# A spline stage on one core: the third power on GpSimd, three quarters of the near part on TensorE, and a new order of the steps

## The chip, the core and the metric

One NeuronCore of a Trainium2 chip runs the whole program. TensorE multiplies matrices, VectorE, ScalarE and GpSimd work elementwise, SyncE (SP) issues most DMAs; each engine runs its own queue in order, and semaphores tie the queues together. The metric is the device time of one launch in microseconds (us), the median of several runs.

## What is computed

`x` is 32 x 64 x 56 x 56, float32. Two 3x3 convolutions with the signs of the weights, each followed by a batch norm, then the residual sum; on its result a cubic spline with 32 knots, whose control values differ by channel (a rank-8 mix). Cut to what matters:

```python
out = relu(batchnorm(conv3x3(x, sign(w1))))
out = relu(batchnorm(conv3x3(out, sign(w2))) + x)          # input v of the spline
u = (clip(v * a + b, -1.5, 1.5) + 1) * 0.5 * 31
i = floor(u); t = clip(u - i, 0, 1)
spline = table[i-1] * b0(t) + table[i] * b1(t) + table[i+1] * b2(t) + table[i+2] * b3(t)
y = id_gain * v + einsum("bchwr,cr->bchw", spline, mix) + bias
```

## The kernel before

A stage of convolutions (to about 408 us of the span) writes its output to scratch memory in HBM. The change lies, but for a few constants, in the second stage, the function `spline`. It handles 32 chunks, each of 128 partitions (two images of 64 channels) by 1568 pixels, half an image pair. Of each pixel, the position on the knots in fixed point (`place`, then `offset`, the signed offset from the next even knot times 2^25, and `cell`, the number of the cell in bfloat16) is formed, and five tables give the coefficients of a polynomial in the offset: T_NEAR, T_FAR, T_SQ, T_LIN, T_VAL. A coefficient is read from its table without a gather: TensorE multiplies 0/1 or sign masks ("is the cell at or above a threshold") by the steps of the table, and so sums up to the right entry. The far term is in |offset| - 1, clipped at 0.

Chunk c passes through these steps. Names are those of the code, lines those of the profile:

- SP: `load(c)` reads y into `lin` (L959); `spread(c)` (L969) waits for `cell_ready` and issues sixteen SBUF to SBUF copies, which lay the cells of 32 channels at a time over all partitions (`cell4`), 98 KB each; `store(c)` (L975) writes `lin` out after `whole`.
- ScalarE: `scale` (L1016), `position` (L1027), `cells` (L1038), `distance` (|offset|, L1064), `far_distance` (L1070), `far_square` (L1076), `distance_square` (L1083), and `edge(c, q)` (L1089), two sign masks of 4 x 1568 columns. `edge` waits on `copied`, that is for all sixteen copies of its chunk.
- VectorE: `fixed` (L1177), `offsets` (L1185), `linear` (L1171), `middle(c, q)` (L1192), the two other masks, which wait for the same copies; then, each reading a table from PSUM, `near_cube` (L1212), `far_cube` (L1219), `square` (L1233), `slope` (L1241), `value` (L1254), and `far_part` (L1226), `add_slope` (L1247) and `finish` (L1261), which read SBUF alone.
- GpSimd: `add_x` (L999) and `add_far` (L1004) issue DMAs that add x and the far part into `lin`.
- TensorE: `table(c, t)` (`product`, L1334), 128 matmuls of 392 columns for each of T_NEAR and T_FAR, 64 for each of the others, and `add_near_part` (L1344), float32 matmuls with the identity `ident` that add `poly` onto the square table in PSUM, for four quarters (`sub`) of the chunk. Two PSUM buffers `tab` alternate: table t waits until table t-2 has been consumed (`table_used`).

The order on each engine is written out by hand. On ScalarE, for chunk index c of the loop: position(c+2), far_distance(c), scale(c+3), far_square(c), distance_square(c), cells(c+2), both edge masks of c+1, distance(c+1). The waits that tie it to the copies are these:

```python
def edge(c, q):
    act.wait_ge(copied[c % 2], copies(c))
def spread(c):
    sp.wait_ge(cell_ready, c + 1)
```

## Time and profile before

| | us |
|---|---|
| median of 3 runs (lowest to highest) | 1127.5 (1126.77 to 1128.81) |
| the profiled execution: its time | 1126.34 |
| its span in the trace | 1124.5 |
| TensorE busy in the span | 1074.4 |
| VectorE busy | 963.5 |
| ScalarE busy | 899.2 |
| GpSimd busy | 170.2 |

The profile is one execution. Busy time counts the instructions of an engine; a matmul record is one pass (float32 matmuls leave two), and the ends of matmuls are modelled. A timeline row merges neighbouring instructions of one kind (x2, x16) and gives start and duration. The duration of a DMA issue on SP is that of issuing; landing is told apart. On ScalarE and VectorE an instruction may start some 0.1 us before its predecessor's end, so start-to-start times are a little shorter than durations.

### The profile page before, as it was taken

What the parts mean: (1) busy time and instruction counts of PE and PEld (TensorE: products, weight loads), DVE (VectorE), ACT (ScalarE), POOL (GpSimd) and SP (SyncE); (2) the same over time, 40 slices, a digit from 0 to 9 for tenths busy, and PEclk for the clock granted to TensorE, in tenths of its full rate; (3) what the DMA queues carried; (4) which work ended last, traced back from release to release, by engine and by line L of the source; (5) the groups of instructions that cost most, each with busy time, mean ns of one, the idle gap of its engine ahead of it and who ended that gap; (6) DMA issues with size and microseconds to landing.
All of it is one profiled execution on the core that took longest, in us unless ns stands there. A gap on an engine that the chain in (4) does not pass through costs nothing.

```text
span 1124.5 us, 53088 instructions
## 1 busy us (share of the span) xinstructions
PE 1074.4 (96%) x24602; PEld 751.0 (67%) x24602; DVE 963.5 (86%) x931; ACT 899.2 (80%) x410; POOL 170.2 (15%) x236
## 2 busy tenths in 40 slices
PE   6999999799999968899999999999999999999996
PEld 5777777687777745566677666666666666666674
DVE  4865666686767779999999999999999999999986
ACT  4444544686777648999999999999999999999970
POOL 8388200000000000111011011110110111101100
PEclk9999999899999989999999999999999999999999
DMA  8577774777677946788888888889988888888642
GB/s 278 216 286 281 278 261 169 266 279 292 252 286 291 350 169 156 191 212 239 227 223 241 219 220 250 218 213 237 230 227 232 230 225 219 235 221 227 169 125 87
DMA packets 57335, 259.43 MB, mean 231 GB/s; under 512 B 15952, under 2 KB 15952, under 8 KB 49104
## 3 DMA queue, kind: packets, MB, share of 16 engines
q1 hardware_dynamic: 48368, 208.39, 52.1%
q0 software_dynamic: 8640, 48.17, 23.6%
q8 instruction: 147, 2.41, 0.9%
q10 hardware_dynamic: 160, 0.30, 0.1%
q14 instruction: 20, 0.16, 0.0%
HBM read 104.28 MB, written 77.07 MB: 161 GB/s over the span
## 4 chain that ended last, share of the span: by engine, by line
PE 94%; DVE 3%; issue 1%; DMA 1%; ACT 0%; ACTq 0%; DVEq 0%
PE tab L1334 52%; PE acc L771 34%; PE tab L1344 8%; DMA w_raw<-in_w 1%; DVE middle_mask L1192 0%; DVE far_sq L1241 0%; PE tab L1356 0%; DVE poly L1233 0%; DVE lin L1276 0%; DVE poly L1272 0%; DVE middle_mask L1201 0%; DVE stats L581 0%; ACT zbuf L1044 0%; DVE edge_mask L1201 0%; DVE offset L1185 0%
## 5 line engine op out<-in xcount | busy, mean ns | idle before, releaser
L1334 PE MATMUL tab<-edge_mask,diag 128*32 128x392 bf16 x10240 | 453.0, 329 | 9.7 <-issue 4.3
L1334 PEld LDWEIGHTS tab<-edge_mask,diag 128*32 128x32 f16 x10240 | 297.5, 97 | 153.5 <-issue 16.3
L1089 ACT ACTIVATE edge_mask<-cell,thr 128x6272 bf16<-128x6272 bf16 x62 | 338.8, 5513 | 2.1 <-DMA cell<-cell 2.1
L472 ACT ACTIVATE yout<-acc 128x1568 f32<-128x1568 f32 x64 | 94.5, 1477 | 162.9 <-PE acc L771 142.3
L771 PE MATMUL acc<-split,w 64*64 64x385 f16 (+3 forms) x4608 | 192.2, 327 | 11.5 <-DVE w L520 10.3
L771 PE MATMUL acc<-band_split,w 64*64 64x385 f16 (+3 forms) x4608 | 192.7, 327 | 6.5 <-DVE band_split L540 3.6
L599 DVE BATCH_NORM_STATS2 stats<-yout 128x392 f32 (+1 forms) x240 | 118.1, 556 | 93.1 <-ACT yout L472 93.1
L1334 PE MATMUL tab<-middle_mask,diag 128*32 128x392 bf16 x4096 | 187.2, 329 | 1.9 <-DVE middle_mask L1201 1.0
L771 PEld LDWEIGHTS acc<-split,w 64*64 64x64 f16 x4608 | 143.9, 108 | 59.0 <-issue 12.8
L771 PEld LDWEIGHTS acc<-band_split,w 64*64 64x64 f16 x4608 | 149.3, 108 | 49.6 <-issue 4.9
L1334 PEld LDWEIGHTS tab<-middle_mask,diag 128*32 128x32 f16 x4096 | 119.2, 97 | 56.7 <-issue 2.4
L1004 POOL DMA_DIRECT2D lin<-far x32 | 50.1, 1564 | 650.4 <-DVE far L1226 650.4
L1192 DVE TENSOR_SCALAR middle_mask<-cell,thr 128x6272 bf16<-128x6272 bf16 x62 | 114.6, 1848 | 0.0
L1344 PE MATMUL tab<-poly,ident 128*32 128x392 f32 x1024 | 92.7, 492 | 0.0
L999 POOL DMA_DIRECT2D lin<-in_x x28 | 32.3, 1153 | 257.7 <-ACT lin L1016 257.7
L1212 DVE SCALAR_TENSOR_TENSOR poly<-tab,first,poly 128x1568 f32<-128x1568 f32 x31 | 57.4, 1851 | 15.6 <-PE tab L1334 15.6
L1344 PEld LDWEIGHTS tab<-poly,ident 128*32 128x32 f32 x1024 | 46.1, 110 | 29.8 <-issue 16.5
L572 DVE SCALAR_TENSOR_TENSOR split<-split,xin 128x3136 f16<-128x3136 f16 (+4 forms) x19 | 55.0, 2907 | 10.1 <-ACT split L462 10.0
L1233 DVE SCALAR_TENSOR_TENSOR poly<-tab,first,dist_sq 128x1568 f32<-128x1568 f32 x31 | 57.3, 1848 | 3.8 <-PE tab L1344 3.6
L1226 DVE SCALAR_TENSOR_TENSOR far<-far,cst,far_sq 128x1568 f32<-128x1568 f32 x32 | 59.3, 1852 | 1.2
L1219 DVE SCALAR_TENSOR_TENSOR far<-tab,first,far 128x1568 f32<-128x1568 f32 x31 | 57.4, 1851 | 2.1 <-PE tab L1334 1.7
L1064 ACT ACTIVATE poly<-offset 128x1568 f32<-128x1568 int32 x32 | 48.4, 1513 | 12.7 <-DVE offset L1185 12.4
(151 smaller groups left out, 1013.7 us busy)
## 6 DMA issues: line engine op xcount, KB each, us to landing
y_scratch<-yout SPq DMA_DIRECT2D x32, 1568.0 KB, 6.1
cell<-cell SPq DMA_DIRECT2D x496, 98.0 KB, 4.0
xin<-y_scratch SPq DMA_DIRECT2D x16, 1568.0 KB, 6.2
lin<-far POOLq DMA_DIRECT2D x32, 784.0 KB, 8.6
out<-lin SPq DMA_DIRECT2D x31, 784.0 KB, 5.0
xin<-in_x SPq DMA_DIRECT2D x15, 1568.0 KB, 6.7
lin<-y_scratch SPq DMA_DIRECT2D x30, 784.0 KB, 8.4
lin<-in_x POOLq DMA_DIRECT2D x28, 784.0 KB, 8.3
```

The costliest lines, as they stand in the source:

```text
L472: act.activation(yout[b][:, :].rearrange("p (r k x) -> p k r x", r=2, k=TILES)[:, 2 * part:2 * part + 2], acc[:, 4 * part:4 * part + 4, 0: ...
L572: dve.scalar_tensor_tensor(out=inner(split[b][1], first, end), in0=inner(split[b][0], first, end), scalar=-SPLIT, in1=rows(xin[b], first, ...
L599: dve.bn_stats(stats[:, bass.ds(COUNTS * (g - base) + t, 1), :], yout[b][:, own]).then_inc(counted, 1)
L771: mm = pe.matmul(to[:, top:end, cols], weights[part][own, tap * C:(tap + 1) * C], image[own, first + dy + top:first + dy + end, from_cols] ...
L1089: act.activation(mask_of(c, q)[:, :, :], cell4[c % 2][:, :, :], ACT.Sign, bias=thr[:, q:q + 1]).then_inc(sign_mask_ready, 1)
L1192: dve.tensor_scalar(mask_of(c, q)[:, :, :], cell4[c % 2][:, :, :], thr[:, q:q + 1], None, ALU.is_ge).then_inc(mask_ready, 1)
L1212: dve.scalar_tensor_tensor(out=quarters(poly[c % 2]), in0=summed(c, T_NEAR), scalar=base(c, T_NEAR), in1=quarters(poly[c % 2]), op0=ALU.ad ...
L1219: dve.scalar_tensor_tensor(out=quarters(far[c % 2]), in0=summed(c, T_FAR), scalar=base(c, T_FAR), in1=quarters(far[c % 2]), op0=ALU.add, o ...
L1226: dve.scalar_tensor_tensor(out=far[c % 2][:, :], in0=far[c % 2][:, :], scalar=cc(AMP), in1=far_sq[:, :], op0=ALU.mult, op1=ALU.mult).then_ ...
L1233: dve.scalar_tensor_tensor(out=quarters(poly[c % 2]), in0=summed(c, T_SQ), scalar=base(c, T_SQ), in1=quarters(dist_sq), op0=ALU.add, op1=A ...
L1334: mm = pe.matmul(tab[(c + t) % 2][j * GROUP:(j + 1) * GROUP, sub, 0:SUB], keep["diag"][part][:, j % 2, t, q, :], mask_of(c, q)[:, j, sub * ...
L1344: mm = pe.matmul(tab[(c + T_SQ) % 2][j * GROUP:(j + 1) * GROUP, sub, 0:SUB], keep["ident"][:, j * GROUP:(j + 1) * GROUP], poly[c % 2][:, s ...
```

## The change

- GpSimd multiplies the clipped far distance by its square (`far_third(c + 1)`, once the middle masks of that chunk are written), one chunk ahead; for chunk 0 VectorE does it. `far_part` goes. The amplitude, made a power of four, enters by its root as the scale of `far_square`, so `add_far` sends what `far_cube` leaves.
- The near table is signed and is multiplied by `offset` instead of |offset|; `ident` holds 2^-25 instead of 1. `distance` writes into `far`.
- TensorE adds the near part for three quarters of a chunk. For the fourth VectorE adds it in the second instruction of `square`, and `rest_of_square` multiplies by the squared distance.
- `slope` writes over `offset`.
- The order is new. ScalarE: position(c+2), scale(c+3), distance_square(c), first edge mask of c+1, distance, far_distance and far_square of c+1, cells(c+2), second edge mask of c+1. VectorE: rest_of_square, add_slope, value and finish of c-1, near_cube(c), offsets(c+1), fixed and linear of c+2, far_cube(c), both middle masks of c+1, square(c), slope(c). SP issues the store ahead of the spread.

The diff, cut to its core (the declarations of the new semaphores are left out):

```diff
-WIDEN = 256.0
+HALF_EXPONENT = 59.5
+PE_QUARTERS = 3
...
-            link(pool.affine_select(out=keep["ident"][:, :], in_=keep["ident"][:, :], compare_op=ALU.not_equal, fill=1.0,
+            link(pool.affine_select(out=keep["ident"][:, :], in_=keep["ident"][:, :], compare_op=ALU.not_equal, fill=1 / POINT,
...
+                bits = amax[:, :].bitcast(I32)
+                link(dve.tensor_scalar(bits, bits, 23, None, ALU.logical_shift_right), chain)
+                link(dve.tensor_scalar(bits, bits, 0.5, HALF_EXPONENT, ALU.mult, ALU.add), chain)
+                link(dve.tensor_scalar(bits, bits, 23, None, ALU.logical_shift_left), chain)
+                link(dve.tensor_copy(col(ROOT_AMP), amax[:, 0:1]), chain)
+                link(dve.tensor_tensor(amax[:, :], amax[:, :], amax[:, :], ALU.mult), chain)
                 link(dve.reciprocal(inv[:, :], amax[:, :]), chain)
-                link(dve.tensor_scalar(inv[:, :], inv[:, :], WIDEN, None, ALU.mult), chain)
                 link(dve.tensor_copy(col(INV_AMP), inv[:, 0:1]), chain)
-                link(dve.tensor_scalar(col(AMP), amax[:, 0:1], 1 / WIDEN, None, ALU.mult), chain)
+                link(dve.tensor_copy(col(AMP), amax[:, 0:1]), chain)
...
-                    link(dve.tensor_tensor(coef[:, :, T_NEAR, at], knots(bend, 1 + 2 * start, count, 4),
-                                           square, ALU.subtract), chain)
+                    beside = knots(bend, 1 + 2 * start, count, 4)
+                    right, left = (square, beside) if start else (beside, square)
+                    link(dve.tensor_tensor(coef[:, :, T_NEAR, at], right, left, ALU.subtract), chain)
...
+        def sloped(c):
+            return offset[c % 2][:, :].bitcast(F32)
...
                 if c + 4 < CHUNKS:
                     load(c + 4)
+                if c > 0:
+                    store(c - 1)
                 if c + 2 < CHUNKS:
                     spread(c + 2)
-                if c > 0:
-                    store(c - 1)
...
+            def far_third(c):
+                pool.wait_ge(mask_ready, dve_masks(c))
+                pool.wait_ge(far_sq_ready, c + 1)
+                pool.tensor_tensor(far[c % 2][:, :], far[c % 2][:, :], far_sq[:, :],
+                                   ALU.mult).then_inc(far_third_ready, 1)
             def add_far(c):
-                pool.wait_ge(far_part_ready, c + 1)
+                pool.wait_ge(table_used, used(c, T_FAR))
+                pool.wait_ge(lin_ready, c + 1)
                 pool.dma_start(lin_of(c)[:, :], far[c % 2][:, :], accum_op=ALU.add).then_inc(far_added, 16)
             for c in range(CHUNKS):
                 if AHEAD <= c + 3 < CHUNKS:
                     add_x(c + 3)
                 add_far(c)
+                if c + 1 < CHUNKS:
+                    far_third(c + 1)
...
             def distance(c):
                 act.wait_ge(offset_ready, c + 1)
-                wait_past(act, whole, c - 1)
-                act.activation(poly[c % 2][:, :], offset[c % 2][:, :], ACT.Abs, scale=1 / POINT).then_inc(dist_ready, 1)
+                wait_past(act, far_added, 16 * (c - 1))
+                act.activation(far[c % 2][:, :], offset[c % 2][:, :], ACT.Abs, scale=1 / POINT).then_inc(dist_ready, 1)
             def far_distance(c):
                 act.wait_ge(dist_ready, c + 1)
-                wait_past(act, far_added, 16 * (c - 1))
-                act.activation(far[c % 2][:, :], poly[c % 2][:, :], ACT.Relu, bias=cc(MINUS_1)).then_inc(far_ready, 1)
+                act.activation(far[c % 2][:, :], far[c % 2][:, :], ACT.Relu, bias=cc(MINUS_1)).then_inc(far_ready, 1)
             def far_square(c):
                 act.wait_ge(far_ready, c + 1)
-                wait_past(act, slope_ready, c)
-                act.activation(far_sq[:, :], far[c % 2][:, :], ACT.Square).then_inc(far_sq_ready, 1)
+                wait_past(act, far_third_ready, c)
+                act.activation(far_sq[:, :], far[c % 2][:, :], ACT.Square, scale=cc(ROOT_AMP)).then_inc(far_sq_ready, 1)
             def distance_square(c):
                 act.wait_ge(offset_ready, c + 1)
-                if c > 0:
-                    act.wait_ge(table_used, used(c - 1, T_SQ))
+                wait_past(act, square_ready, c)
                 act.activation(dist_sq[:, :], offset[c % 2][:, :], ACT.Square, scale=1 / POINT).then_inc(dist_sq_ready, 1)
             def edge(c, q):
             for q in EDGE_QUADS:
                 edge(1, q)
             distance(1)
+            far_distance(1)
+            far_square(1)
             for c in range(1, CHUNKS):
                 if c + 2 < CHUNKS:
                     position(c + 2)
-                far_distance(c)
                 if AHEAD <= c + 3 < CHUNKS:
                     scale(c + 3)
-                far_square(c)
                 distance_square(c)
+                if c + 1 < CHUNKS:
+                    edge(c + 1, EDGE_QUADS[0])
+                    distance(c + 1)
+                    far_distance(c + 1)
+                    far_square(c + 1)
                 if c + 2 < CHUNKS:
                     cells(c + 2)
                 if c + 1 < CHUNKS:
-                    for q in EDGE_QUADS:
-                        edge(c + 1, q)
-                    distance(c + 1)
+                    edge(c + 1, EDGE_QUADS[1])
...
             def near_cube(c):
-                dve.wait_ge(far_ready, c + 1)
+                dve.wait_ge(offset_ready, c + 1)
+                wait_past(dve, whole, c - 1)
                 dve.wait_ge(table_ready, used(c, T_NEAR))
                 dve.scalar_tensor_tensor(out=quarters(poly[c % 2]), in0=summed(c, T_NEAR), scalar=base(c, T_NEAR),
-                                         in1=quarters(poly[c % 2]), op0=ALU.add, op1=ALU.mult).then_inc(table_used, 1)
+                                         in1=quarters(offset[c % 2]), op0=ALU.add, op1=ALU.mult).then_inc(table_used, 1)
+            def first_far_third():
+                dve.wait_ge(far_sq_ready, 1)
+                dve.tensor_tensor(far[0][:, :], far[0][:, :], far_sq[:, :], ALU.mult).then_inc(far_third_ready, 1)
             def far_cube(c):
-                dve.wait_ge(far_sq_ready, c + 1)
+                dve.wait_ge(far_third_ready, c + 1)
                 dve.wait_ge(table_ready, used(c, T_FAR))
                 dve.scalar_tensor_tensor(out=quarters(far[c % 2]), in0=summed(c, T_FAR), scalar=base(c, T_FAR),
                                          in1=quarters(far[c % 2]), op0=ALU.add, op1=ALU.mult).then_inc(table_used, 1)
-            def far_part(c):
-                dve.wait_ge(table_used, used(c, T_FAR))
-                dve.wait_ge(lin_ready, c + 1)
-                dve.scalar_tensor_tensor(out=far[c % 2][:, :], in0=far[c % 2][:, :], scalar=cc(AMP), in1=far_sq[:, :],
-                                         op0=ALU.mult, op1=ALU.mult).then_inc(far_part_ready, 1)
             def square(c):
+                most, rest = slice(0, PE_QUARTERS), slice(PE_QUARTERS, 4)
                 dve.wait_ge(dist_sq_ready, c + 1)
+                dve.wait_ge(table_used, used(c, T_NEAR))
                 dve.wait_ge(table_ready, used(c, T_SQ))
-                dve.scalar_tensor_tensor(out=quarters(poly[c % 2]), in0=summed(c, T_SQ), scalar=base(c, T_SQ),
-                                         in1=quarters(dist_sq), op0=ALU.add,
-                                         op1=ALU.mult).then_inc(table_used, 1)
+                dve.scalar_tensor_tensor(out=quarters(poly[c % 2])[:, most, :], in0=summed(c, T_SQ)[:, most, :],
+                                         scalar=base(c, T_SQ), in1=quarters(dist_sq)[:, most, :], op0=ALU.add,
+                                         op1=ALU.mult).then_inc(square_parts, 1)
+                dve.scalar_tensor_tensor(out=quarters(poly[c % 2])[:, rest, :], in0=quarters(poly[c % 2])[:, rest, :],
+                                         scalar=1 / POINT, in1=summed(c, T_SQ)[:, rest, :], op0=ALU.mult,
+                                         op1=ALU.add).then_inc(table_used, 1)
+            def rest_of_square(c):
+                own = slice(PE_QUARTERS * SUB, CHUNK)
+                dve.wait_ge(table_used, used(c, T_SQ))
+                dve.scalar_tensor_tensor(out=poly[c % 2][:, own], in0=poly[c % 2][:, own], scalar=base(c, T_SQ),
+                                         in1=dist_sq[:, own], op0=ALU.add, op1=ALU.mult).then_inc(square_ready, 1)
             def slope(c):
-                dve.wait_ge(far_part_ready, c + 1)
+                dve.wait_ge(dist_ready, c + 1)
+                dve.wait_ge(dist_sq_ready, c + 1)
+                dve.wait_ge(table_used, used(c, T_NEAR))
                 dve.wait_ge(table_ready, used(c, T_LIN))
-                dve.scalar_tensor_tensor(out=quarters(far_sq), in0=summed(c, T_LIN), scalar=base(c, T_LIN),
+                dve.scalar_tensor_tensor(out=quarters(sloped(c)), in0=summed(c, T_LIN), scalar=base(c, T_LIN),
                                          in1=quarters(offset[c % 2]), op0=ALU.add, op1=ALU.mult).then_inc(table_used, 1)
             def add_slope(c):
                 dve.wait_ge(table_used, used(c, T_LIN))
-                dve.scalar_tensor_tensor(out=poly[c % 2][:, :], in0=far_sq[:, :], scalar=1 / POINT,
+                dve.wait_ge(square_parts, c + 1)
+                dve.wait_ge(square_ready, c + 1)
+                dve.scalar_tensor_tensor(out=poly[c % 2][:, :], in0=sloped(c), scalar=1 / POINT,
                                          in1=poly[c % 2][:, :], op0=ALU.mult, op1=ALU.add).then_inc(slope_ready, 1)
             def value(c):
             near_cube(0)
             fixed(2)
             total(3)
+            first_far_third()
             far_cube(0)
             linear(0)
-            far_part(0)
             middle(1, MIDDLE_QUADS[0])
             square(0)
             offsets(1)
             slope(0)
             middle(1, MIDDLE_QUADS[1])
+            rest_of_square(0)
             add_slope(0)
             value(0)
             linear(1)
             linear(2)
             for c in range(1, CHUNKS):
                 if c > 1:
+                    rest_of_square(c - 1)
+                    add_slope(c - 1)
                     value(c - 1)
+                finish(c - 1)
+                near_cube(c)
+                if c + 1 < CHUNKS:
+                    offsets(c + 1)
                 if c + 2 < CHUNKS:
                     fixed(c + 2)
                     linear(c + 2)
-                near_cube(c)
-                finish(c - 1)
+                far_cube(c)
                 if c + 1 < CHUNKS:
-                    middle(c + 1, MIDDLE_QUADS[0])
-                far_cube(c)
-                far_part(c)
-                if c + 1 < CHUNKS:
-                    middle(c + 1, MIDDLE_QUADS[1])
+                    for q in MIDDLE_QUADS:
+                        middle(c + 1, q)
                 square(c)
-                if c + 1 < CHUNKS:
-                    offsets(c + 1)
                 slope(c)
-                add_slope(c)
+            rest_of_square(CHUNKS - 1)
+            add_slope(CHUNKS - 1)
             closing_quarters()
...
-                                       stop=(t != T_SQ and q == QUADS_OF[t][-1] and part == 1))
+                                       stop=((t != T_SQ or sub >= PE_QUARTERS) and q == QUADS_OF[t][-1] and part == 1))
...
                 if t == T_SQ:
                     pe.wait_ge(table_used, used(c, T_NEAR))
-                    for sub in range(4):
+                    for sub in range(PE_QUARTERS):
```

## Rows read from the trace of the kernel before

**Rows 1.** The page, busy totals (us, share, count) and DMA issues (count, size, us to landing).

```profile
PE 1074.4 (96%) x24602; PEld 751.0 (67%) x24602; DVE 963.5 (86%) x931; ACT 899.2 (80%) x410; POOL 170.2 (15%) x236
...
lin<-far POOLq DMA_DIRECT2D x32, 784.0 KB, 8.6
```

**Rows 2.** Busy time by stretch: PE, PEld, DVE, ACT, POOL, then clock, DMA share, GB/s.

```profile
465.00:485.00 20.00, 16.68 (x404) 10.94 (x396) 19.04 (x13) 20.00 (x10) 2.45 (x2) 1.00 0.84 210
800.00:1000.00 200.00, 198.77 (x4496) 133.17 (x4488) 194.59 (x121) 198.41 (x84) 24.93 (x18) 1.00 0.88 228
```

**Rows 3.** The chain that ended last, 780 to 900 us: start, duration, what.

```profile
853.19 18.57 PE tab L1334 x448
871.76 2.63 PE tab L1344 x32
```

**Rows 4.** Waits, 560 to 1100 us: total, times, longest.

```profile
ACT poly L1064 <- DVE offset L1185: 10.7, 9, 4.6
```

**Rows 5.** Timeline of one chunk, about 500 to 516 us: start, duration, engine, line, operation.

```profile
499.69 1.50 ACT L1083 ACTIVATE dist_sq<-offset 128x1568 f32<-128x1568 int32 x1
...
501.10 1.59 ACT L1038 ACTIVATE cell<-zbuf,cst 128x1568 bf16<-128x1568 uint16 x1
...
502.71 14.12 SPq L969 DMA_DIRECT2D cell<-cell  x16
...
507.21 1.85 DVE L1226 SCALAR_TENSOR_TENSOR far<-far,cst,far_sq 128x1568 f32<-128x1568 f32 x1
...
508.98 1.85 DVE L1192 TENSOR_SCALAR middle_mask<-cell,thr 128x6272 bf16<-128x6272 bf16 x1
...
513.50 1.52 ACT L1064 ACTIVATE poly<-offset 128x1568 f32<-128x1568 int32 x1
514.91 1.68 ACT L1027 ACTIVATE zbuf<-lin,cst 128x1568 f32<-128x1568 f32 x1
...
516.50 1.59 ACT L1070 ACTIVATE far<-poly,cst 128x1568 f32<-128x1568 f32 x1
```

**Rows 6.** The tile `cell`, 824 to 838 us: its sixteen copies.

```profile
DMA to landing us min/median/max: 2.6/4.3/6.7
```

**Rows 7.** Timeline, VectorE on a quarter chunk at the end.

```profile
1117.47 0.63 DVE L1276 SCALAR_TENSOR_TENSOR lin<-poly,cst,lin 128x392 f32<-128x392 f32 x1
```

**Rows 8.** Timeline, opening of the spline stage, 423 to 450 us.

```profile
423.21 1.60 ACT L1038 ACTIVATE cell<-zbuf,cst 128x1568 bf16<-128x1568 uint16 x1 [0.27 <-DVE zbuf L1177]
...
424.90 11.55 SPq L969 DMA_DIRECT2D cell<-cell  x16
...
437.90 14.63 SPq L969 DMA_DIRECT2D cell<-cell  x16
...
438.97 10.94 ACT L1089 ACTIVATE edge_mask<-cell,thr 128x6272 bf16<-128x6272 bf16 x2 [2.13 <-DMA cell<-cell]
```

**Rows 9.** Timeline, the last spread of cells, and the transfer that follows.

```profile
1058.01 10.28 SPq L969 DMA_DIRECT2D cell<-cell  x16
...
1065.94 1.59 POOL L1004 DMA_DIRECT2D lin<-far  x1 [19.62 <-DVE far L1226]
```

**Rows 10.** The tile `cell`, 1058 to 1068 us: issue ns (min/median/max) and landing.

```profile
L969 SPq DMA_DIRECT2D cell<-cell x16: 469/596/727, 1058.0 to 1067.7; - x16
...
DMA to landing us min/median/max: 2.2/2.5/6.9
```

**Rows 11.** Groups by line, GpSimd: busy us, mean ns.

```profile
L389 POOL TENSOR_TENSOR w_signs<-w_signs,w_below 128x576 f32<-128x576 f32 x1 | 1.4, 1412 | 0.1
```

**Rows 12.** Timeline, VectorE and GpSimd, 65 to 71 us.

```profile
65.25 0.21 POOL L344 TENSOR_TENSOR dsel<-dsel,own_step 128x10 f32<-128x10 f32 x1
...
66.82 3.43 DVE L572 SCALAR_TENSOR_TENSOR split<-split,xin 128x3136 f16<-128x3136 f16 x1 [0.61 <-ACT split L462]
66.83 3.55 POOL L347 TENSOR_TENSOR dlo<-dsel,dhi 128x40 f32<-128x40 f32 x1
```

**Rows 13.** Timeline, TensorE after the first half of the last chunk's tables.

```profile
1099.41 2.98 PE L1334 MATMUL tab<-middle_mask,diag 128*32 128x392 bf16 x64
```

8 lines of the change are left out of this document (5 added, 3 removed).

## The prediction

> **What bounds the kernel now.** I read the engine totals first, then the busy table by stretch, the chain, the waits, and last the timeline of one chunk. TensorE is busy 96% of the span, VectorE 86%, ScalarE 80% [rows 1]. The change touches only the spline stage, so its own stretch counts: in 800 to 1000 us TensorE is busy 198.8 of 200 us, but ScalarE 198.4 and VectorE 194.6 [rows 2]. The chain runs through TensorE alone, in a period of 18.57 + 2.63 = 21.20 us for a chunk [rows 3]: 448 products at 0.041 us, and the 32 records of the near part at 0.082 us. The waits say how far the others are off: ScalarE waits 10.7 us in 25 chunks, in nine of them [rows 4]. So three engines share one period, TensorE by a hair.
>
> There is a fourth party, which the totals hide: the copies that spread the cells. In one chunk of the timeline ScalarE writes the cells at 501.10, ends at 502.69, SP issues 16 copies from 502.71 on for 14.12 us, and only after the last has landed may the edge masks of that chunk start, one period later [rows 5]. A copy lands 4.3 us after its issue in such a stretch [rows 6], so the cells are spread about 14.1 + 4.3 - 0.6 = 17.8 us after they were written, and ScalarE has 21.2 us of other work between. It is hidden with 3.4 us to spare, so no view of waits names it.
>
> **Part by part.**
>
> *Near part on TensorE.* 24 of 32 records stay: 8 x 0.082 = 0.66 us less of each chunk, 31 chunks, 20 us if TensorE alone set the period.
>
> *VectorE.* `far_part` goes: 1.77 us from its start to the next start (507.21 to 508.98) [rows 5]. `square` in two pieces and `rest_of_square` are three instructions for 392 x 5 columns instead of one for 392 x 4; a 392-column one takes 0.63 us [rows 7], some 0.55 from start to start, as long ones overlap by 0.08 too. That is +0.1 for the split and +0.5 for the last quarter. VectorE goes from 0.973 x 21.2 = 20.6 to about 19.4 us a chunk. But the order puts both middle masks ahead of `square(c)`: `far_cube` starts 10.9 us after TensorE began the chunk (10.6 of tables and 0.3), then 1.8 + 1.8 + 1.8, so `square` starts at 16.3, where the shorter table would be there at 15.6; it frees the bank 2.0 later, at 18.3, 0.4 after TensorE wants it at 17.9. So the period can't be 20.5 but about 21.0, whatever ScalarE does.
>
> *ScalarE.* Same eight kinds of instructions. `far_square` gets a scale from memory: by the rows with one such operand (1.59 us, `cell`) and none (1.50, `dist_sq`) that is +0.09 [rows 5]. Its work is 21.2 - 0.2 of waiting + 0.1 = 21.1 us a chunk.
>
> *The new order on ScalarE, the term that decides.* Each instruction that moves: `distance`, `far_distance`, `far_square` of c+1 now stand between the two edge masks, and `cells(c+2)` behind them, ahead of the second mask only. Before, `cells(c+2)` stood ahead of both masks of c+1. Between `cells(c+2)` and `edge(c+2, 0)`, which waits for the sixteen copies of those same cells, there is left: one mask 5.5 (half of the pair's 10.94 [rows 8]), `position` 1.6, `scale` 1.5, `distance_square` 1.4, together 10.0 us, not 21.2 less one instruction. The copies need more than that, and now they are in a ring: edge mask 0 of c+1 (5.4), `distance` 1.4, `far_distance` 1.5, `far_square` 1.5, `cells` 1.6 = 11.4 us, then D, the time from the cells to the last copy's landing, then edge mask 0 of c+2. **Period P = 11.4 + D**, for as long as D is over 10.0. Behind the waiting mask are queued on ScalarE the distance, its powers, the next cells and the second mask, and TensorE's first table needs that mask; on VectorE the middle masks wait for the same copies.
>
> *What is D?* Three rows, none of them under the new order. In steady state 17.8, as above, but there the accumulating transfer `lin<-far` (issued 6 to 7 us into the copies) and others overlap it. In the opening, ScalarE did wait for the copies: cells written at 424.81, issue 424.90 for 11.55, first edge mask at 438.97, so D = 14.2, of which 2.5 follow the last issue [rows 8]. Near the end, with nothing beside it for its first 8 us, the issue takes 10.28 and `lin<-far` comes only at 1065.94 [rows 9]. The shortest single issue is 0.47 and the shortest landing 2.6 in a loaded stretch, 2.2 in the light one [rows 6, 10]: 16 x 0.47 + 2.4 = 9.9 is the floor. Which applies? Roll one period from S, the start of edge mask 0 of c+1, at P near 24: cells end S + 11.4, second mask S + 16.8, `scale(c+4)` S + 19.9, its GpSimd transfer from S + 20.2; TensorE's first table waits for the second mask and ends S + 18.4, far table S + 23.7, `far_cube` ends S + 25.8, that is 1.6 us into the next period, so `lin<-far` (8.6 us [rows 1]) lands about S + 10.5, just before the next copies start. The load and the store of SP go out behind the copies. So the copies run almost alone, as at 1058. D = 10.3 + 2.5 = 12.8, **P = 24.2 us**.
>
> *GpSimd's multiplication.* The trace has no such row in this stage. From below: VectorE's two-input row of that shape, 1.85. From above: GpSimd's 576 columns in 1.41 us make 3.8 for 1568 [rows 11]. I take 3.8. It starts at S + 9.9 (after `far_square`), `far_cube` needs it at S + 23.9, and `far_square` of the next chunk later still, so it costs nothing while P is 24; without that cover its cost is a rival below. It stands on GpSimd's queue ahead of `add_x(c+4)`, which is asked for at S + 19.9, 6 us later.
>
> *One answer each.* Four more small instructions for the scale in the opening, 0.2 us each, beside a convolution whose statistics wait anyway; 0.8 if that cover is gone. The signed near table, the different constants, the store ahead of the spread (SP's queue is empty then): nothing.
>
> *Sum.* The opening first. In the profile the masks of chunk 1 begin at 438.97 and end at 449.9 [rows 8]; the same eight instructions reordered bring ScalarE to edge mask 0 of chunk 2 at 449.8 + 1.4 + 1.5 + 1.5 + 1.6 + 1.5 + 1.4 = 458.7 (its copies, issued 437.90 to 452.53, land by 455.0, so no wait). Chunks 3 to 31 each follow the ring: 29 P. Tail: from edge mask 0 of chunk 31 to the end of its first table 5.4 + 1.4 + 1.5 + 1.5 + 5.5 + 0.1 + 1.3 = 16.7; before, that point (1099.4) was 25.1 us ahead of the end of the span [rows 13]; less 0.1, since VectorE sets the very end and `rest_of_square` gives back most of the 0.66: 25.0. Span = 458.7 + 41.7 + 29 x 24.2 = 1202.2. The profiled execution took 1126.34 for a span of 1124.5, so 1.8 us lie around it, and the median of the runs is 1.2 above it: **1205.2 us**.
>
> **Rivals.**
>
> *The copies stay slow* (D up to 17.8, the steady row). If the `add_x` transfer or the load behind the copies catches their last few, landing goes from 2.4 to 6.9 us, as the last copies at 1058 show [rows 10]. Then P = 26 to 29.2 and the time is 1257 to 1350. For it: those late landings came 8 us into the copies, and here `add_x` comes 8.8 us in. Against: at 0.6 us an issue the last copy is out at S + 21. The Trainium skill, page "DMA: Bandwidth & Descriptors", section "Queues, rings and completion order", has each transfer engine take turns between the queues that have work for it; by that rule copies that meet a GpSimd transfer are halved in rate, which is this rival, and it speaks for it wherever they meet.
>
> *The ring closes in time* (faster). Place: the wait of `edge(c+2, 0)`. It is hidden if D is under 10.0, for which all sixteen issues must take the shortest row's 0.47. Then ScalarE's 21.1 and the late `square`, 21.0, set the period: 0.1 x 30 = 3 us less, 1124; if those two were off as well, TensorE's 0.66 x 31, 1107. For it: rows of 0.47 exist. Against: the median issue even in the light stretch is 0.596 [rows 10].
>
> *GpSimd and VectorE block one another* (slower), with the copies in time. Row: a GpSimd subtraction of 40 columns, started 0.01 us after a 3.43 us VectorE instruction with two inputs in SBUF, took 3.55 us; one of 10 columns a little earlier, beside VectorE's statistics, took 0.21 [rows 12]. In this kernel `add_slope`, `finish` and `rest_of_square` have two such inputs. If the multiplication meets them and holds them for its whole 3.8 us, VectorE's chunk is 19.4 + 3.8 = 23.2, a period 2.0 over today's: 1127.5 + 30 x 2.0 = 1188. It decides once 19.4 plus the overlap exceeds the ring's P. The Trainium skill, page "SBUF — State Buffer", says in its section "Who interferes with whom" that contention arises at the shared port pair alone and that it is an exclusive lock; the row agrees (3.55 against 3.43).
>
> *The change doesn't do what it says.* The near part does get cheaper, but if that shows nowhere because another wait is last, the near part's line shrinks and the period doesn't: contained in all of the above.
>
> **How the numbers follow.** Forecast, ring with copies nearly alone, D between 11.4 and 14.2, 1165 to 1246 us: 0.66. Copies slow, 1246 to 1350: 0.20. Blocking decides, about 1188: 0.06. Ring closes in time: 0.08, of it 0.06 faster and 0.02 within 0.2%, about what a measurement of this kernel tells from no change. Slower 0.92. The range runs from D = 11.4 (1165) to P = 27.1 (1290), leaving out half of the slow-copy case and the fast one.
>
> **What would show it.** Right: ScalarE's first edge mask waits some 3 us a chunk for the DMA of the cells, 90 us in all; the near part's group has 24 records a chunk; TensorE idles about 3.5 us a chunk; the chain passes through cells, copies and edge mask. Wrong: if that wait is absent or the copies land within 10 us of the cells; if TensorE's clock falls in the new gaps (at 465 to 485 it idled 3.3 of 20 us at full clock [rows 2]); if the wait is there, but D isn't 12.8, only the term D was off.

## The result and the profile after

| | before | after |
|---|---|---|
| median of the runs, us | 1127.13 (4 runs) | 1335.71 (1333.49 to 1335.85, 4 runs) |
| ratio to before | | 1.1848, 95% interval 1.1824 to 1.1873 |
| the profiled execution, us | 1126.34 | 1335.61 |
| its span | 1124.5 | 1333.8 |

The changed kernel is 208.6 us slower. The forecast was 1205.2 us, with a range to 1290: the direction was right, the size was not. The time is in the case that was given 0.20, copies that stay slow.

Experiments 2 to 6 below stand on one run each; their granted clocks (0.932 to 0.958) are like those of the kernel after (0.932 to 0.938), and none is near the 0.558 of the one slow run on record, so they are read as fast.

The page of the kernel after, its busy totals and the chain that ended last (against [rows 1, 3]):

```profile
PE 1120.6 (84%) x24346; PEld 735.4 (55%) x24346; DVE 995.2 (75%) x968; ACT 908.1 (68%) x410; POOL 267.1 (20%) x267
...
PE 30%; SPq 21%; issue 17%; DMA 16%; ACT 13%; DVE 2%; ACTq 1%; DVEq 0%
PE acc L778 29%; SPq L982 21%; DMA cell<-cell 15%; ACT far L1092 4%; ACT cell L1061 4%; ACT far L1087 3%; ACT edge_mask L1110 1%; PE tab L1375 1%; ACTq L1458 1%; DMA w_raw<-in_w 0%; PE tab L1397 0%; DVE lin L1315 0%; DVE poly L1311 0%; DVE stats L582 0%; ACT zbuf L1067 0%
```

TensorE made up 94% of the chain; now the spline's tables (L1375) are 1% of it. In their place stand SP issuing the copies of the cells (L982), the landing of the last copy, and steps of ScalarE. Most of the 17% of "issue" is ScalarE too: the view of the chain puts 5.41 us of each turn, the time of the first edge mask itself, under that name (its last line below). No engine is busy for more than 84% of the span. In the waits (who waited for whom: total, times, longest; 560 to 1250 us) the mask that waits for the copies is the first that does not belong to GpSimd (against [rows 4], where it is missing):

```profile
ACT edge_mask L1110 <- DMA cell<-cell: 176.0, 24, 8.4
...
PE tab L1375 <- ACT edge_mask L1110: 115.0, 24, 4.9
DVE poly L1237 <- PE tab L1375: 109.4, 24, 4.6
```

One turn of the ring in the timeline of the kernel after (start, duration, what), against the chunk of [rows 5]:

```profile
806.44 5.53 ACT L1110 ACTIVATE edge_mask<-cell,thr 128x6272 bf16<-128x6272 bf16 x1 [7.02 <-DMA cell<-cell]
...
811.87 1.50 ACT L1087 ACTIVATE far<-offset 128x1568 f32<-128x1568 int32 x1
...
813.40 1.60 ACT L1092 ACTIVATE far<-far,cst 128x1568 f32<-128x1568 f32 x1
...
815.04 1.60 ACT L1098 ACTIVATE far_sq<-far,cst 128x1568 f32<-128x1568 f32 x1
...
816.55 1.59 ACT L1061 ACTIVATE cell<-zbuf,cst 128x1568 bf16<-128x1568 uint16 x1
...
818.16 10.05 SPq L982 DMA_DIRECT2D cell<-cell  x16
...
826.93 0.88 POOL L1012 DMA_DIRECT2D lin<-in_x  x1 [6.62 <-ACT lin L1039]
...
834.64 5.52 ACT L1110 ACTIVATE edge_mask<-cell,thr 128x6272 bf16<-128x6272 bf16 x1 [6.61 <-DMA cell<-cell]
```

From mask to mask 28.2 us: 11.7 to the end of the cells (818.14), then D = 16.5. Over all turns (1290.12, the last first mask, less 458.81, the one of chunk 2, by 29) the period is 28.7. The chain of the same stretch names what the end of D is made of:

```profile
827.58 0.04 issue
827.62 7.00 DMA cell<-cell
834.62 0.02 issue
834.64 0.02 ACT edge_mask L1110
834.66 5.41 issue
```

The issue of the sixteenth copy starts at 827.62, and it lands 7.00 us later, 6.4 us after its issue has ended (818.16 + 10.05 = 828.21). The view of the tile `cell`, first over all sixteen copies (818 to 829 us), then over the first fourteen (818 to 826.9 us), against [rows 6, 10]:

```profile
L982 SPq DMA_DIRECT2D cell<-cell x16: 476/595/600, 818.2 to 827.6; - x16
...
DMA to landing us min/median/max: 2.2/2.3/7.0
...
DMA to landing us min/median/max: 2.2/2.3/2.4
```

The issue is as fast as in the lightest stretch of before (median 595 ns), the median landing too (2.3 us). Late are the last copies alone: the fifteenth, issued 0.05 us after the transfer `lin<-in_x` (826.93), took 3.2 us, the sixteenth, issued 0.69 us after it, 7.0. Other turns vary: in the 23 that start between 560 and 1250 us the issue takes 10.0 to 12.5 us (10.8 on the mean), and from its end to the last landing it is 4.7 to 7.6 us (6.3 on the mean).

### The profile page after: what moved, and what is told of

Its sections match the earlier page's. It is cut to its first block, busy times and chain, and to the rows that moved or that the text cites. A ratio compares the mean times of both kernels' runs of the same rounds, so it can differ in the third digit from the quotient of the medians.

```text
span 1333.8 us, 52709 instructions
## 1 busy us (share of the span) xinstructions
PE 1120.6 (84%) x24346; PEld 735.4 (55%) x24346; DVE 995.2 (75%) x968; ACT 908.1 (68%) x410; POOL 267.1 (20%) x267
## 4 chain that ended last, share of the span: by engine, by line
PE 30%; SPq 21%; issue 17%; DMA 16%; ACT 13%; DVE 2%; ACTq 1%; DVEq 0%
PE acc L778 29%; SPq L982 21%; DMA cell<-cell 15%; ACT far L1092 4%; ACT cell L1061 4%; ACT far L1087 3%; ACT edge_mask L1110 1%; PE tab L1375 1%; ACTq L1458 1%; DMA w_raw<-in_w 0%; PE tab L1397 0%; DVE lin L1315 0%; DVE poly L1311 0%; DVE stats L582 0%; ACT zbuf L1067 0%
## 5 line engine op out<-in xcount | busy, mean ns | idle before, releaser
L1375 PE MATMUL tab<-edge_mask,diag 128*32 128x392 bf16 x10240 | 490.1, 347 | 170.7 <-ACT edge_mask L1110 133.5
L1375 PEld LDWEIGHTS tab<-edge_mask,diag 128*32 128x32 f16 x10240 | 275.6, 101 | 370.0 <-ACT edge_mask L1110 144.9
L1375 PE MATMUL tab<-middle_mask,diag 128*32 128x392 bf16 x4096 | 205.9, 358 | 1.9 <-DVE middle_mask L1225 1.0
L778 PE MATMUL acc<-band_split,w 64*64 64x385 f16 (+2 forms) x4608 | 192.1, 327 | 7.3 <-issue 3.7
L778 PEld LDWEIGHTS acc<-split,w 64*64 64x64 f16 x4608 | 167.2, 108 | 35.4 <-issue 12.5
L1375 PEld LDWEIGHTS tab<-middle_mask,diag 128*32 128x32 f16 x4096 | 119.5, 107 | 85.0 <-issue 34.4
L1018 POOL TENSOR_TENSOR far<-far,far_sq 128x1568 f32<-128x1568 f32 x31 | 109.3, 3526 | 282.2 <-ACT far_sq L1098 280.5
L1237 DVE SCALAR_TENSOR_TENSOR poly<-tab,first,offset 128x1568 f32<-128x1568 f32 x31 | 57.4, 1851 | 126.0 <-PE tab L1375 126.0
L1216 DVE TENSOR_SCALAR middle_mask<-cell,thr 128x6272 bf16<-128x6272 bf16 x62 | 112.4, 1854 | 25.2 <-DMA cell<-cell 25.1
L1300 DVE SCALAR_TENSOR_TENSOR lin<-poly,cst,lin 128x1568 f32<-128x1568 f32 x31 | 112.4, 3626 | 1.1
L1385 PE MATMUL tab<-poly,ident 128*32 128x392 f32 x768 | 69.0, 492 | 0.0
L573 DVE SCALAR_TENSOR_TENSOR split<-split,xin 128x3136 f16<-128x3136 f16 (+4 forms) x19 | 55.0, 2910 | 10.1 <-ACT split L463 10.1
L1286 DVE SCALAR_TENSOR_TENSOR poly<-offset,poly 128x1568 f32<-128x1568 f32 x32 | 57.4, 1793 | 4.5
L1278 DVE SCALAR_TENSOR_TENSOR offset<-tab,first,offset 128x1568 f32<-128x1568 f32 x31 | 57.2, 1844 | 1.8 <-PE tab L1375 1.5
## 6 DMA issues: line engine op xcount, KB each, us to landing
out<-lin SPq DMA_DIRECT2D x31, 784.0 KB, 10.1
```

What stands on the lines that cost most here:

```text
L778: mm = pe.matmul(to[:, top:end, cols], weights[part][own, tap * C:(tap + 1) * C], image[own, first + dy + top:first + dy + end, from_cols] ...
L1018: pool.tensor_tensor(far[c % 2][:, :], far[c % 2][:, :], far_sq[:, :], ALU.mult).then_inc(far_third_ready, 1)
L1216: dve.tensor_scalar(mask_of(c, q)[:, :, :], cell4[c % 2][:, :, :], thr[:, q:q + 1], None, ALU.is_ge).then_inc(mask_ready, 1)
L1237: dve.scalar_tensor_tensor(out=quarters(poly[c % 2]), in0=summed(c, T_NEAR), scalar=base(c, T_NEAR), in1=quarters(offset[c % 2]), op0=ALU. ...
L1300: dve.scalar_tensor_tensor(out=lin_of(c)[:, :], in0=poly[c % 2][:, :], scalar=cc(AMP), in1=lin_of(c)[:, :], op0=ALU.mult, op1=ALU.add).the ...
L1375: mm = pe.matmul(tab[(c + t) % 2][j * GROUP:(j + 1) * GROUP, sub, 0:SUB], keep["diag"][part][:, j % 2, t, q, :], mask_of(c, q)[:, j, sub * ...
```

## The experiments

They go by the questions that the traces left: is it the ring at all (1, 2), what makes the last copies late (3 to 5), and what is left of the change without the ring (6 to 9).

**1. Cells back ahead of the masks** (kernel after, one step moved back).

```diff
                 distance_square(c)
+                if c + 2 < CHUNKS:
+                    cells(c + 2)
                 if c + 1 < CHUNKS:
                     edge(c + 1, EDGE_QUADS[0])
                     distance(c + 1)
                     far_distance(c + 1)
                     far_square(c + 1)
-                if c + 2 < CHUNKS:
-                    cells(c + 2)
-                if c + 1 < CHUNKS:
                     edge(c + 1, EDGE_QUADS[1])
```

> The changed kernel with one step moved back: cells(c+2) stands ahead of the first edge mask of c+1 on ScalarE, as it did before. Ring theory: between the cells and the mask that waits for their copies there are then 19.5 us of ScalarE's own work, more than the 16.9 us that the copies take in the changed kernel, so the wait of the edge mask for the DMA of the cells (212 us in all) goes to nearly nothing, and ScalarE's own 21.1 us set the period: 1124 us, between 1119 and 1135. Rival, GpSimd's multiplication and VectorE block one another (finish takes 3.63 us for 1.84): VectorE's chunk is 19.4 + 1.8 to 3.8, a period of 21.2 to 23.2, 1128 to 1188 us. Rival, the new work or TensorE's lower clock is at fault: over 1250 us still.

Measured: 1174.27 us, ratio 1.0449 (1.0408 to 1.0490). The wait for the copies has gone, 0.2 us in 560 to 1140 us:

```profile
ACT cell L1061 <- DVE zbuf L1200: 29.2, 25, 2.9
...
ACT edge_mask L1110 <- DMA cell<-cell: 0.2, 1, 0.2
```

One instruction's place was worth 161 us of the 209. But 1124 was wrong: 49 us are left, and the first row above points at the next wait, `cells` for `fixed`. The timeline shows it as a second ring, from one second edge mask to the next: the mask holds the first table, the table `near_cube` (L1236), then come `offsets`, `fixed` (L1200), the cells, the first mask and the three powers, 22.60 us around. ScalarE is not idle ahead of the mask at 821.72. The view of the chain puts TensorE ahead of it, but the tables that `edge` waits for there, those of the chunk before, were done by 804:

```profile
799.12 5.50 ACT L1110 ACTIVATE edge_mask<-cell,thr 128x6272 bf16<-128x6272 bf16 x1
...
806.34 1.85 DVE L1236 SCALAR_TENSOR_TENSOR poly<-tab,first,offset 128x1568 f32<-128x1568 f32 x1 [0.63 <-PE tab L1374]
...
808.98 1.09 DVE L1200 TENSOR_SCALAR zbuf<-zbuf,cst 128x1568 int32<-128x1568 f32 x1
...
810.11 1.61 ACT L1061 ACTIVATE cell<-zbuf,cst 128x1568 bf16<-128x1568 uint16 x1 [1.01 <-DVE zbuf L1200]
...
821.72 5.51 ACT L1110 ACTIVATE edge_mask<-cell,thr 128x6272 bf16<-128x6272 bf16 x1
```

**2. The reverse: the kernel before with only that step moved.**

```diff
+                if c + 1 < CHUNKS:
+                    edge(c + 1, EDGE_QUADS[0])
                 if c + 2 < CHUNKS:
                     cells(c + 2)
                 if c + 1 < CHUNKS:
-                    for q in EDGE_QUADS:
-                        edge(c + 1, q)
+                    edge(c + 1, EDGE_QUADS[1])
                     distance(c + 1)
```

> The kernel before with the one step moved the other way: cells(c+2) stands between the two edge masks of c+1, all else as before. Ring theory: between the cells and the mask that waits for them ScalarE has 5.5 + 1.4 + 1.6 + 1.5 + 1.5 + 1.4 + 1.4 = 14.3 us of other work in place of 19.8, and the ring is 5.4 + 1.6 + D. With D = 16.9 as in the changed kernel the period is 23.9, the mask waits 2.7 us a chunk, and the time is about 1127 + 29 x 2.7 = 1205 us; with D between 14.3 and 17.8 it is 1127 to 1232. Without such a ring (rival: the loss is in the other parts of the change) 1127 us and no wait of the edge mask.

Measured: 1305.18 us, outside of what was expected, on the slow side. The ring is there without any other part of the change, so it is the order that makes it. What was expected took D from the kernel after; here it is longer. The timeline gives it: cells written 801.29, next first mask 822.67, so 21.4 us.

```profile
800.07 1.59 POOL L1004 DMA_DIRECT2D lin<-far  x1 [14.56 <-DVE far L1227]
...
801.31 16.13 SPq L969 DMA_DIRECT2D cell<-cell  x16
...
812.97 0.86 POOL L999 DMA_DIRECT2D lin<-in_x  x1 [11.31 <-ACT lin L1016]
...
822.67 5.52 ACT L1089 ACTIVATE edge_mask<-cell,thr 128x6272 bf16<-128x6272 bf16 x1 [7.19 <-DMA cell<-cell]
```

Here both GpSimd transfers lie over the copies, one at their start and one at their end, and D is longer than in any row of before: the issue takes 16.13 us, and the last copy lands 5.2 us after its end.

**3. Without the transfers that add x** (kernel after).

```diff
-                    act.wait_ge(x_added, 16 * (c - AHEAD + 1))
+                    act.wait_ge(scaled, c - AHEAD + 1)
...
-                if AHEAD <= c + 3 < CHUNKS:
-                    add_x(c + 3)
                 add_far(c)
```

> The changed kernel without the 28 GpSimd transfers that add x into lin (the outputs of chunks 4 to 31 lack x). It asks why the last copies land 6 to 7 us after their issue and not 2.4. If add_x, which starts 8.8 us after the first copy, slows them: D falls from 16.9 to 10.3 + 2.5 = 12.8, the period to 11.6 + 12.8 = 24.4, the time to 458.8 + 41.7 + 29 x 24.4 + 1.8 = 1210 us. If the load and the store that SP issues right behind the copies slow them: D and time stay, 1335 us. Both together: in between, 1250 to 1300.

Measured: 1235.09 us. From the first mask of chunk 2 (459.49) to that of chunk 31 (1189.62), by 29, the period is 25.2, so D = 13.5 on the mean. The longest landing of a copy in 800 to 850 us is 3.4:

```profile
DMA to landing us min/median/max: 2.2/2.4/3.4
```

D varies: in one turn it is 12.5 us (cells written at 799.8, mask at 812.30), in the next 14.9:

```profile
824.02 12.19 SPq L982 DMA_DIRECT2D cell<-cell  x16
...
838.89 5.52 ACT L1108 ACTIVATE edge_mask<-cell,thr 128x6272 bf16<-128x6272 bf16 x1 [5.00 <-DMA cell<-cell]
```

There two of the sixteen issues take 1.64 and 1.67 us instead of 0.60. It isn't `lin<-far` (issued 816.70) that meets them, since that transfer has landed 7.1 us later, at 823.8, before the first copy goes out; what holds them is not shown. Of the 209 us lost, 100 hang on this one transfer's being there.

The kernel after holds the same experiment in itself. In its last two spreads no chunk is left whose x must be added, and no load either. D falls to 12.7 us in the first of them (cells written 1252.26) and 13.5 in the second, and `add_far` and the store are still there:

```profile
1250.67 1.59 ACT L1061 ACTIVATE cell<-zbuf,cst 128x1568 bf16<-128x1568 uint16 x1
...
1264.92 5.53 ACT L1110 ACTIVATE edge_mask<-cell,thr 128x6272 bf16<-128x6272 bf16 x1 [4.27 <-DMA cell<-cell]
```

**4. The load and the store of SP held until the copies have landed** (kernel after).

```diff
             for c in range(CHUNKS):
+                if 0 < c < CHUNKS - 1:
+                    sp.wait_ge(sign_mask_ready, edge_masks(c) + 1)
                 if c + 4 < CHUNKS:
                     load(c + 4)
```

> The changed kernel with the load and the store on SP held until the first edge mask of the chunk is done, so until the copies have landed; add_x is left alone. If the load and the store behind the copies slow the last of them: D falls from 16.9 to 12.8 and the time to 1210 us. If add_x slows them: D stays 16.9 and the time 1335 us (or a little more, as the load comes 7 us later, of which its reader has 12 to spare).

Measured: 1349.37 us, 1% over the kernel after. The load and the store now go out ahead of the copies (817.25 and 817.63) and have landed by 824.7 (5.5 and 7.1 us later); the copies start at 823.41, and nothing of SP's is in flight behind them. The last of them is late all the same (tile `cell`, 823 to 836 us; then the last copy alone):

```profile
L982 SPq DMA_DIRECT2D cell<-cell x16: 476/595/1455, 823.4 to 833.7; - x16
...
DMA to landing us min/median/max: 2.3/2.3/8.3
...
DMA to landing us min/median/max: 8.3/8.3/8.3
```

What SP queues behind the copies is not what makes the last one late. The edit is not free of a side effect: in their new place the load and the store can meet the first copies, and the issue took 11.8 us on the mean for 10.8 (turns of 560 to 1250 us).

**5. The same transfer at another time** (kernel after, `scale` and with it `add_x` a mask later).

```diff
-                if AHEAD <= c + 3 < CHUNKS:
-                    scale(c + 3)
                 distance_square(c)
                 if c + 1 < CHUNKS:
                     edge(c + 1, EDGE_QUADS[0])
+                    if AHEAD <= c + 3 < CHUNKS:
+                        scale(c + 3)
                     distance(c + 1)
```

> The changed kernel with scale(c+3) moved behind the first edge mask, so that its GpSimd transfer starts 4 to 6 us ahead of the copies rather than 8.8 us into them. e3 showed that without that transfer the period is 25.3 and not 28.7. Theory, its place matters: scale adds 1.5 us to the ring (13.1 us), but the last copies land in 2.4 us again, D = 12.8 to 14.5, the period is 25.9 to 27.6 and the time 458.8 + 41.7 + 29 P + 1.8 = 1253 to 1303 us. Rival, its bytes cost the same wherever they go: D = 16.9, the period 30.0, the time 1372 us.

Measured: 1306.47 us, 3 us above the range of the theory and far below the rival's 1372. One turn:

```profile
831.36 12.71 SPq L982 DMA_DIRECT2D cell<-cell  x16
...
846.52 5.53 ACT L1110 ACTIVATE edge_mask<-cell,thr 128x6272 bf16<-128x6272 bf16 x1 [6.79 <-DMA cell<-cell]
```

The ring's own part grew by `scale` to 13.2 us. D is 15.2 in this turn, one of the longer ones; over all turns (first masks from 457.22 to 1261.46, by 29) the period is 27.7, so D = 14.5 on the mean, for 17.0 in the kernel after. The last copy lands 2.5 us after the end of the issue again, as expected, but the issue now takes 12.7 us in place of 10.1: `lin<-in_x` and `lin<-far` go out together at 825.5 and 826.1, and the first copies, which meet them, land after 4.8 us. So the place matters, for 2.5 us of D on the mean, of which `scale` in the ring takes 1.5 back. A transfer that is moved off the last copies lies over the first.

**6. GpSimd's multiplication cut to 16 columns** (kernel after).

```diff
-                pool.tensor_tensor(far[c % 2][:, :], far[c % 2][:, :], far_sq[:, :],
+                pool.tensor_tensor(far[c % 2][:, 0:16], far[c % 2][:, 0:16], far_sq[:, 0:16],
```

> The changed kernel with GpSimd's multiplication cut to 16 of 1568 columns (the far part of the other columns of chunks 1 to 31 is left without its square). It prices the multiplication and the blocking of VectorE. Ring theory: finish falls from 3.63 us to 1.84, and the time stays at 1335 us (1325 to 1340), since nothing of it lies in the ring. Rival, blocking is part of the loss: 1335 - 29 x 1.8 = 1283 us.

Measured: 1340.38 us, no gain, while `finish` fell from 3.83 to 1.85 us on the mean (groups by line, 560 to 1200 us; first the kernel after, then this one):

```profile
L1300 DVE SCALAR_TENSOR_TENSOR lin<-poly,cst,lin 128x1568 f32<-128x1568 f32 x23 | 88.0, 3828 | 0.8
```

```profile
L1300 DVE SCALAR_TENSOR_TENSOR lin<-poly,cst,lin 128x1568 f32<-128x1568 f32 x22 | 40.8, 1852 | 0.8
```

The blocking is real, 2.0 us a chunk, and under the ring it costs nothing.

**7. The second ring: `fixed` ahead of `near_cube`** (on top of experiment 1).

```diff
                 finish(c - 1)
+                if c + 2 < CHUNKS:
+                    fixed(c + 2)
                 near_cube(c)
                 if c + 1 < CHUNKS:
                     offsets(c + 1)
                 if c + 2 < CHUNKS:
-                    fixed(c + 2)
                     linear(c + 2)
```

> The kernel of e1 (cells ahead of both masks) with fixed(c+2) moved ahead of near_cube(c) on VectorE. e1 took 1174 us with a period of 22.6: the wait for the copies is gone, but cells(c+2) waits 1.0 us a chunk for fixed(c+2), which stands behind near_cube(c), which needs the first table, which needs the second mask of c: a second ring, 10.99 us from that mask's start to the cells plus 11.61 from the cells to the next second mask = 22.6. If this is the cause of e1's loss, the wait of cells for VectorE goes and the period falls to ScalarE's own 21.6: 1174 - 30 x 1.0 = 1144 us, 1138 to 1152. Rival, GpSimd's multiplication blocks VectorE (finish takes 3.13 us in e1 for 1.84 before) and that sets e1's period: 1174 us still.

Measured: 1161.2 us, ratio 1.0310 (1.0287 to 1.0333): 13 us of the 30 expected. The wait of `cells` for `fixed` is still 24.5 us, but now VectorE is what the chain runs through (its shares by engine, then the timeline around `rest_of_square`, L1268):

```profile
DVE 50%; PE 37%; issue 11%; DMA 1%; DVEq 0%; ACT 0%; ACTq 0%
...
809.84 5.51 ACT L1110 ACTIVATE edge_mask<-cell,thr 128x6272 bf16<-128x6272 bf16 x1
810.08 3.53 POOL L1018 TENSOR_TENSOR far<-far,far_sq 128x1568 f32<-128x1568 f32 x1 [4.59 <-ACT far_sq L1098]
810.63 3.40 DVE L1268 SCALAR_TENSOR_TENSOR poly<-poly,first,dist_sq 128x392 f32<-128x392 f32 x1
```

An instruction that takes 0.62 us in the kernel after (L1269, mean of 22) takes 3.40 here, where GpSimd began 0.55 us earlier; the two end 0.4 us apart (813.61 and 814.03). VectorE is busy 198.1 of 200 us in this kernel (800 to 1000 us). The rival that was to be ruled out, blocking, looks like what stands behind the second ring; experiments 8 and 9 test it.

**8. The powers ahead of the masks** (on top of experiment 7), so that the multiplication falls beside `square` and `slope`.

```diff
-                distance_square(c)
                 if c + 2 < CHUNKS:
                     cells(c + 2)
+                distance_square(c)
                 if c + 1 < CHUNKS:
-                    edge(c + 1, EDGE_QUADS[0])
                     distance(c + 1)
                     far_distance(c + 1)
                     far_square(c + 1)
+                    edge(c + 1, EDGE_QUADS[0])
                     edge(c + 1, EDGE_QUADS[1])
```

> The kernel of e5 with ScalarE's order cells(c+2), distance_square(c), distance, far_distance, far_square of c+1, and then both edge masks. GpSimd's multiplication can then begin when the middle masks are written, beside square and slope of VectorE, which read PSUM, and not beside rest_of_square (3.40 us for 0.62 in e5). If the blocking sets e5's period of 22.5: rest_of_square returns to 0.62, the period falls to ScalarE's own 21.6 and the time to 1161 - 30 x 0.9 = 1134 us, 1128 to 1142. Rival, VectorE's load or the late masks set it: 1155 us or more.

Measured: 1134.87 us, ratio 1.0066 (1.0046 to 1.0087). In its groups by line `rest_of_square` is at its own length, with the multiplication in full:

```profile
L1268 DVE SCALAR_TENSOR_TENSOR poly<-poly,first,dist_sq 128x392 f32<-128x392 f32 x25 | 15.5, 618 | 0.0
```

**9. The multiplication cut to 16 columns** on top of experiment 7, the edit that was worth nothing in the changed kernel.

```diff
-                pool.tensor_tensor(far[c % 2][:, :], far[c % 2][:, :], far_sq[:, :],
+                pool.tensor_tensor(far[c % 2][:, 0:16], far[c % 2][:, 0:16], far_sq[:, 0:16],
```

> The kernel of e5 with GpSimd's multiplication cut to 16 of 1568 columns (the far part of the rest of chunks 1 to 31 is left without its square). The price of the blocking by itself, where the copies' ring is open. If blocking sets the period: rest_of_square 0.62 us, period 21.6, 1134 us, 1128 to 1142. If not: 1161 us. In the changed kernel the same cut changed nothing, 1340 us.

Measured: 1129.22 us, ratio 1.0002 (0.9984 to 1.0019). With the ring open the same edit is worth 32 us, the price of the blocking. Experiment 8 keeps the multiplication in full and gets all but 6 us of that by ScalarE's order alone.

What bounds experiment 8 is ScalarE. Its busy time by stretch (PE, PEld, DVE, ACT, POOL; against [rows 2]):

```profile
800.00:1000.00 200.00, 195.02 (x4396) 122.40 (x4392) 184.76 (x131) 199.38 (x84) 55.00 (x28) 1.00 0.89 225
```

TensorE is busy 195.0 us for 198.8 and VectorE 184.8 for 194.6, and neither is the bound. ScalarE is busy all but 0.6 of the 200 us, and with the same eight kinds of instructions it comes around in 21.5 us (from one `position` at 849.24 to the next at 870.72), where the kernel before took 21.2. None of the versions beats the kernel before.

## Why the prediction was right or wrong

- **The mechanism, right.** The ring of cells, copies and first mask is the chain of the kernel after in the spline stage, and experiments 1 and 2 show it from both sides: taken out of the kernel after it gives back 161 us, put into the kernel before it costs 180.
- **The opening and the tail.** First mask of chunk 2 forecast for 458.7, measured 458.81. From the first mask of chunk 31 to the end of the span 43.7, forecast 41.7.
- **11.4, ScalarE's part of the ring: 11.7.** The starts of the three powers and of the cells behind them lie 1.53, 1.64 and 1.51 us apart, where 1.4, 1.5 and 1.5 were taken from rows in which neighbours overlap. The two that grew, 1.53 and 1.64, are those in which an instruction reads what the one just ahead of it wrote.
- **D = 12.8, the step that failed.** It measured 16.5 in the turn above, and 28.7 - 11.7 = 17.0 on the mean. Its first part was nearly right: issue 10.05 us in that turn and 10.8 on the mean, for 10.3. The tail, from the end of the issue to the last landing, was not: 2.5 us taken, 6.4 in that turn and 6.3 on the mean. The roll of the period put the `add_x` transfer at S + 20.2 and the last copy at S + 21; they came at S + 20.5 and S + 21.2. From these numbers the text concluded that the copies run "almost alone", and gave the rows that said otherwise, landings up to 6.9 us when a GpSimd transfer starts 2 us before the end of the copies [rows 9, 10], to a rival. Those rows were the better precedent: the same transfer size, 8 us into the copies. More than that, the 10.3 and the 2.5 were put together from two places. The issue came from the spread at 1058, the tail from the opening; the spread at 1058 taken whole has its last copy out at 1067.7 and landed 6.9 us later, so 16.6 us from the cells (1058.0), which is what the kernel after measured. Experiment 3 confirms the transfer as the cause; without it D is 13.5 on the mean (12.5 and 14.9 in the turns above), near the 12.8, and the time 1235. With D = 17.0 the prediction's own sum gives 500.4 + 29 x 28.4 + 3 = 1327, and 1336 with the 11.7. This is no second proof, as the 17.0 is taken from the period; it says how the error is shared out, 4.2 us a turn by D and 0.3 by ScalarE's part.
- **The rule on turns between queues.** The section "Queues, rings and completion order" of the Trainium skill's page "DMA: Bandwidth & Descriptors" has the queues of a transfer engine take turns. The rule was used as a factor of two on copies that meet the transfer. The trace agrees that they meet and are slowed, but not on one factor: for 2.3 us alone, the fifteenth copy took 3.2 and the sixteenth 7.0. The sixteenth landed (834.6) about when the transfer did that was issued 0.7 us before it and took 8.5 us (835.4).
- **GpSimd's multiplication, and the blocking.** The multiplication took 3.52 us for the 3.8 taken. Blocking was given 0.06 as what decides, at about 1188 us, and was costed at nothing under the ring. Experiment 6 shows the nothing. Experiments 7 and 9 show the rival, in the condition that was named for it, copies in time: 1161 us, and 1129 with the multiplication cut. It held up `finish` in the kernel after and `rest_of_square` in experiment 7, both with two inputs in SBUF. The section "Who interferes with whom" of the Trainium skill's page "SBUF — State Buffer" says that a VectorE instruction with two SBUF inputs contends with a GpSimd one that reads SBUF; 3.40 us for 0.62 agrees.
- **The near part and VectorE.** 24 records a chunk for 32 as forecast (768 in all), and the first piece of `square` takes 1.44, the second 0.55, the last quarter 0.62 us. All hidden.
- **The sign that was given for wrong.** The prediction named a fall of TensorE's clock in the new gaps as a sign against it. The clock did fall, to 0.90 on the mean of 800 to 1200 us; it is told below. It wasn't what cost the time: the spline's tables are 1% of the chain. The last sign named, the wait is there but D isn't 12.8, is what came.
- **The case that the ring closes in time (1124), wrong in its size.** Experiment 1 took the copies out of the ring by hand and measured 1174. Two things behind the ring had not been seen: the second ring of experiment 1, which runs through the second edge mask, put behind the three powers, and through `fixed`, put behind `near_cube`; and the blocking behind that. With both gone (experiments 8 and 9) the time is 1135 and 1129.

## What to carry to other kernels

When a step is moved on one engine, follow what it starts on other queues to the first instruction that waits for it, and compare the work left between the two with the time the round trip takes: here 10.0 us against 17, where 21.2 against 17.8 had been enough to hide it from every view of waits. Take that time from one row with the same neighbours at the same moment, and take it whole, the last landing above all, since a wait for sixteen copies is a wait for the slowest. And after one bound is lifted, expect the next: three stood one behind the other here (the time went from 1336 to 1174, 1161 and 1135 us), and an edit that was worth nothing under the first was worth 32 us under the last.

## What the hardware showed that was not expected

- A copy of 98 KB that is issued 0.7 us after an accumulating GpSimd transfer of 784 KB lands about when the transfer does: 7.0 us for 2.3. In 22 of 26 turns of the kernel after (500 to 1250 us) the last copy landed within 1.2 us of `lin<-in_x`, in the others up to 2.6 us from it. Why it waits that long is not shown. With such a transfer at the start and another at the end, sixteen copies took 21.4 us (experiment 2); with none at the end 12.2 to 15.9 (experiments 3 and 5, 560 to 1250 us).
- TensorE's granted clock. It stood idle from 818.75 to 823.61, waiting for the second mask, and the clock went to 0.50, the lower level of 1.2 GHz, within that gap; it is full again in the row of 830 to 832 us. At the lower level 32 products took 2.81 us (at 823.61), at full clock 1.50 (at 817.25). Granted clock is the third number from the end:

```profile
816.00:818.00 2.00, 2.00 (x56) 1.29 (x52) 1.96 (x2) 2.00 (x2) 1.21 (x1) 1.00 0.06 12
818.00:820.00 2.00, 0.75 (x20) 0.24 (x12) 1.97 (x1) 2.00 (x2) 2.00 (x1) 1.00 0.26 58
820.00:822.00 2.00, 0.00 (x0) 0.00 (x0) 1.96 (x1) 2.00 (x1) 0.31 (x1) 0.93 0.62 158
822.00:824.00 2.00, 0.39 (x8) 0.23 (x12) 0.00 (x0) 2.00 (x2) 0.00 (x0) 0.50 0.53 152
...
826.00:828.00 2.00, 2.00 (x32) 1.01 (x28) 1.44 (x1) 2.00 (x2) 0.88 (x1) 0.50 0.61 158
...
830.00:832.00 2.00, 2.00 (x59) 1.24 (x52) 1.31 (x2) 0.00 (x0) 0.00 (x0) 1.00 1.03 207
```

  In the kernel before, 465 to 485 us, TensorE idled 3.3 of 20 us in pieces of at most 2.6 us, and the clock stayed full [rows 2]. In the kernel after the mean over 800 to 1200 us was 0.90. It cost nothing here, TensorE being off the chain. It did not fall so in the tighter versions: 1.00 over 800 to 1000 us in experiments 7 and 8.
